# A fused conditioning, two-layer ternary feed-forward and 4-bit rounding kernel: block 1 conditioned inside block 0's first product, and one 8 KB buffer for the small conditioning tiles

## The reference

```
w = weights[conditions];  c = einsum('bct,bcd->bdt', x, w)
ternarize(W): delta = 0.05*max|W|; mask = |W|>delta; alpha = sum(|W| mask)/max(sum(mask),1); alpha*sign(W)*mask
h = gelu(c @ ternarize(W1).T + b1)            # 512 -> 2048
y = h @ ternarize(W2).T + b2                  # 2048 -> 512
scale = max|y|/7 + 1e-8;  q = clip(round(y/scale), -7, 7)*scale
out = x + q
```

## Time and profile before

| | us |
|---|---|
| median of 3 runs | 1014.92 (1014.45 to 1015.22) |
| the profiled execution | 1013.76 |
| its span | 1012.0 |
| block 0's first product begins | 33.08 |
| its second product begins | 66.13 |
| block 1's first product begins | 97.21 |
| the loop's period | 57.12 |
| the maximum of y is known | 954.94 |

### The profile page before, as it was taken

The page is one execution under the profiler, slowest core; times in us unless marked ns, Lnnn a source line. Parts: engine busy times, 40 slices in busy tenths (PEclk is TensorE's granted clock), DMA queues, the critical chain, the costliest instruction groups (busy, mean ns, idle before and its releaser), DMA issues.

```text
span 1012.0 us, 14566 instructions
## 1 busy us (share of the span) xinstructions
PE 928.2 (92%) x5088; PEld 439.1 (43%) x5088; DVE 647.5 (64%) x1025; ACT 546.2 (54%) x688; POOL 145.4 (14%) x187
## 2 busy tenths in 40 slices
PE   2899999999999999999999999999999999999600
PEld 2354444444444444444444444444444444444200
DVE  7999666566667666665667666565666665633492
ACT  5685826455472827446372827446372826535290
POOL 1420030210303030110303030110303030000000
PEclk9999999999999999999999999999999999999855
DMA  9401201111210301121210301121210301105899
GB/s 347 136 9 38 46 11 42 47 47 41 52 41 17 76 10 41 46 47 41 52 41 10 83 10 41 45 48 41 52 41 10 75 18 42 42 0 201 300 394 391
DMA packets 24317, 77.85 MB, mean 77 GB/s; under 512 B 3952, under 2 KB 4080, under 8 KB 23792
## 3 DMA queue, kind: packets, MB, share of 16 engines
q1 hardware_dynamic: 20032, 73.41, 24.1%
q0 software_dynamic: 3840, 3.94, 1.4%
q10 hardware_dynamic: 432, 0.34, 0.1%
HBM read 60.89 MB, written 16.78 MB: 77 GB/s over the span
## 4 chain that ended last, share of the span: by engine, by line
PE 83%; issue 9%; DVE 4%; ACT 1%; DMA 1%; DVEq 0%; POOL 0%; POOLq 0%
PE ps L426 41%; PE ps L436 36%; PE ps L491 3%; PE ps L406 3%; ACT y L680 1%; DVE st L814 1%; DVE wts L1017 1%; DMA condb<-in_itok_B 1%; DVE y L1017 0%; DVE y L833 0%; PE ps L414 0%; PE ps L454 0%; DVE yc L746 0%; DVEq L58 0%; DVE st L697 0%
## 5 line engine op out<-in xcount | busy, mean ns | idle before, releaser
L426 PE MATMUL ps<-yc,wts 128*128 128x512 f16 x2048 | 446.3, 380 | 3.6 <-DVE yc L746 3.6
L436 PE MATMUL ps<-wts 128*128 128x512 f16 x1792 | 391.4, 379 | 0.0
L426 PEld LDWEIGHTS ps<-yc,wts 128*128 128x128 f16 x2048 | 200.7, 98 | 246.8 <-DVE yc L746 4.1
L730 DVE SCALAR_TENSOR_TENSOR wts<-g,st,wts 128x512 f16<-128x512 f32 x256 | 186.3, 749 | 144.0 <-ACT wts L593 142.4
L588 ACT ACTIVATE g<-ps,b1t,st 128x512 f32<-128x512 f32 x256 | 197.9, 773 | 129.0 <-PE ps L426 120.7
L436 PEld LDWEIGHTS ps<-wts 128*128 128x128 f16 x1792 | 173.4, 98 | 204.9
L593 ACT ACTIVATE wts<-g,st 128x512 f16<-128x512 f32 x256 | 180.8, 712 | 0.0
L575 ACT ACTIVATE xs<-yx,st 128x2048 f16<-128x2048 f32 x28 | 56.1, 2002 | 135.5 <-DVE st L764 135.5
L359 POOL PARTITION_ALL_REDUCE st<-st x46 | 22.7, 494 | 672.5 <-DVE st L699 412.7
L343 POOL DMA_INDIRECT wg<-in_L_cond_weights,ids x112 | 110.0, 982 | 41.5 <-issue 29.1
L735 DVE SCALAR_TENSOR_TENSOR y<-ps,st,b2b 128x512 f32 (+1 forms) x56 | 41.6, 747 | 78.9 <-PE ps L436 78.1
(11 more groups left out here) (127 smaller groups left out, 359.3 us busy)
## 6 DMA issues: line engine op xcount, KB each, us to landing
yx<-in_x SPq DMA_DIRECT2D x56, 512.0 KB, 6.2
out<-wts SPq DMA_DIRECT2D x12, 512.0 KB, 14.9
wts<-in_x SPq DMA_DIRECT2D x10, 512.0 KB, 5.6
y<-in_L_ffn_W SPq DMA_DIRECT2D x8, 512.0 KB, 8.6
wts<-in_x SPq DMA_DIRECT2D x4, 1024.0 KB, 5.2
y<-in_L_ffn_W SPq DMA_DIRECT2D x4, 1024.0 KB, 18.5
y<-in_x SPq DMA_DIRECT2D x4, 1024.0 KB, 10.7
out<-y SPq DMA_DIRECT2D x4, 1024.0 KB, 15.3
```

Of the source, the lines that this page charges most:

```text
L426: last = nc.tensor.matmul(psH[:, j % HB, :], T1T[:, j // HC, k, j % HC * P:(j % HC + 1) * P], csp[:, a, k, :], start=(k == 0 and a == 0), ...
L436: last = nc.tensor.matmul(psY[:, r % 2, :], hsp[:, a, j, r * P:(r + 1) * P], T2T[:, j, :], start=(j == 0 and a == 0), stop=(j == HT - 1 an ...
L730: nc.vector.scalar_tensor_tensor(out=hsp[:, 1, j, :], in0=g[:, j % HB, :], scalar=s_h, in1=hsp[:, 0, j, :], op0=ALU.mult, op1=ALU.subtract ...
```

## The change

The diff does this:

- The small buffers (`wg`, `ws`, `condb`, `idx`, `ids`, `idsd`, `twos`) become slices of one buffer `odd` of 8 KB for each partition; in the end it takes block 1 of x, so 13 blocks of x are loaded before the maximum and 3 after. Every later block moves one place.
- Block 1's conditioning on PE stands behind tile 0 of block 0's first product. Its copy goes to a buffer of its own (`cf1`), beside GELU of tiles 3 and 5; ACT's `relu2(0)` stands behind GELU of tile 11. The gathers, `spread_w(1)` and x's load for it come earlier.
- DVE no longer takes the maximum of block 0's x; ACT takes the sum of |x| in each partition in its place (`dump_x`). Two memsets stand ahead of a wait.
- `count2` counts with the masks as the stationary side and one column of `twos` as the moving side: 64 matmuls in place of 16.
- DVE's order beside block 0's two products is new, and `low_x(0, 0)` stands behind the four `max_y` instead of ahead of the four `store_y`.

```diff
-twos = sb("twos", [P, P], FP16)
...
+odd = sb("odd", [P, RT * T], FP32)
+wg = odd[:, 0:BB * C].rearrange("p (b d) -> p b d", b=BB)
+ws = odd[:, BB * C:2 * BB * C].bitcast(FP16).rearrange("p (a b d) -> p a b d", a=2, b=BB)
+odd_i = odd[:, 2 * BB * C:].bitcast(I32)
+condb, idx, ids = odd_i[:, 0:B], odd_i[:, B:2 * B], odd_i[:, 2 * B:2 * B + BB]
+idsd = odd_i[:, 2 * B + BB:2 * B + BB + DIRECT * RT].rearrange("p (b r) -> p b r", b=DIRECT)
+twos = odd[:, 3 * BB * C:3 * BB * C + P // 2].bitcast(FP16)
...
-       10: [(slice(m, m + 1), ALL) for m in (0, 1)],
-       11: [(slice(m, m + 1), ALL) for m in (0, 1)]}
+       11: [(slice(m, m + 1), ALL) for m in (0, 1)],
+       12: [(slice(m, m + 1), ALL) for m in (0, 1)]}
...
-mask1, neg2, dump2 = f16(y[:, 12:14, :, :]), f16(y[:, 4:6, :, :]), f16(y[:, 0:4, :, :])
+mask1, neg2, dump2 = f16(y[:, 12:14, :, :]), f16(y[:, 6:8, :, :]), f16(y[:, 0:4, :, :])
...
+cf1 = y[:, 4, :, :]
+dump_x = hsp[:, 0, 0:RT, :].rearrange("p j r -> p (j r)")
...
-xtail = [place(xs[:, :, :].rearrange("p b t -> p (b t)").bitcast(FP32)),
+xtail = [place(xs[:, :, :].rearrange("p b t -> p (b t)").bitcast(FP32)), place(odd[:, :]),
...
-xhalf = {10: [parts[:, 2, 2:3, :, :], parts[:, 0:2, 3, 0:1, :].rearrange("p w n t -> p n w t")],
-         11: [parts[:, 2, 3:4, :, :], parts[:, 0:2, 3, 1:2, :].rearrange("p w n t -> p n w t")]}
-APART = (6, 8, 9, 10, 11)
+xhalf = {11: [parts[:, 2, 2:3, :, :], parts[:, 0:2, 3, 0:1, :].rearrange("p w n t -> p n w t")],
+         12: [parts[:, 2, 3:4, :, :], parts[:, 0:2, 3, 1:2, :].rearrange("p w n t -> p n w t")]}
+APART = (7, 9, 10, 11, 12)
...
-psC1 = psH[:, 0:2, :].rearrange("p i (k r) -> p (i k) r", k=KT // 2)
-psN1, psN2 = psH[:, HB - 1, :], ps[:, HB, :]
+psN1, psN2 = psH[:, HB - 1, :], ps[:, HB, 0:1]
...
     load_direct(0)
+    load_direct(1)
     load_weight(w2s, W2.rearrange("p j n -> p (j n)"), WCH, w2_loaded)
-    load_direct(1)
...
     sp.wait_ge(c_made, 2 * NB)
-    load_tail(0)
+    for b in range(2):
+        load_tail(b)
     sp.wait_ge(h_summed, NB * HT - HT // 2)
-    load_tail(1)
+    load_tail(2)
     sp.wait_ge(h_summed, NB * HT)
-    for b in range(2, 4):
+    for b in range(3, 5):
         load_tail(b)
...
-    def gather_direct(b):
-        for r in range(RT):
+    def gather_direct(b, tiles):
+        for r in tiles:
...
     pool.wait_ge(idx_made, 1)
-    gather_direct(0)
+    gather_direct(0, range(RT))
+    gather_direct(1, range(0, 2))
...
     all_max(max1_part, 1, m1r, m1, max1_all)
+    gather_direct(1, range(2, RT))
+    pool.wait_ge(x0_summed, 1)
     all_max(xwb_part, 1, xwbr, xwb, xwb_all)
-    gather_direct(1)
     pool.wait_ge(sum1_part, 1)
     nc.gpsimd.partition_all_reduce(rs1r, rs1s, P, RADD).then_inc(sum1_all, 1)
     pool.wait_ge(w_spread, DIRECT)
...
-    all_max(xw_part, 1, xwr, xw, xw_all)
     pool.wait_ge(sum2_part, 1)
     nc.gpsimd.partition_all_reduce(sum2r, sum2, P, RADD).then_inc(sum2_all, 1)
+    all_max(xw_part, 1, xwr, xw, xw_all)
...
     def count2(c):
-        for n in range(WCH):
-            last = nc.tensor.matmul(psN2, twos[:, :], quarter(neg2, c, n), start=(c == 0 and n == 0),
-                                    stop=(c == WCH - 1 and n == WCH - 1))
+        for n in range(QUARTER // P):
+            at = c * QUARTER + n * P
+            last = nc.tensor.matmul(psN2, neg2[:, at:at + P], twos[:, 0:1], start=(c == 0 and n == 0),
+                                    stop=(c == WCH - 1 and n == QUARTER // P - 1))
...
         first(0, j, wait_bank=j >= HB, wait_c=False)
-
-    pe.wait_ge(xdirect_loaded[1], 16)
-    pe.wait_ge(w_spread, 2)
-    condition_direct(1, 0, psC)
-    pe.wait_ge(g_made, HT - 2)
-    condition_direct(1, 1, psC1)
-
+        if j == 0:
+            pe.wait_ge(xdirect_loaded[1], 16)
+            pe.wait_ge(w_spread, 2)
+            condition_direct(1, 0, psC)
+            condition_direct(1, 1, psC0)
+
+    pe.wait_ge(c_copied, 2)
     pe.wait_ge(g_made, HT)
...
         if j == 3 * HC:
-            pe.wait_ge(c_copied, 1)
             for c in range(WCH):
                 count2(c)
...
-    for c in range(6):
+    for c in range(LOADS):
         absolute(c)
+    act.dma_start(b2b[:, :], b2.rearrange("(a n) -> a n", a=1).to_broadcast([P, T])).then_inc(b2_loaded, 16)
     act.wait_ge(diagonal_cleared, 1)
     spread_w(0)
-    for c in range(6, LOADS):
-        absolute(c)
-    act.dma_start(b2b[:, :], b2.rearrange("(a n) -> a n", a=1).to_broadcast([P, T])).then_inc(b2_loaded, 16)
+    act.wait_ge(xdirect_loaded[0], 16)
+    nc.scalar.activation(dump_x, xdirect[0].rearrange("p r t -> p (r t)"), ACT.Abs, accum_out=xwb[:, 0:1])\
+        .then_inc(x0_summed, 1)
     act.wait_ge(delta1_ready, 1)
     act.wait_ge(w1abs_made, LOADS)
-    for c in range(3):
-        relu1(c)
+    relu1(0)
     high_c0(0, psC)
     high_c0(1, psC0)
+    relu1(1)
+    act.wait_ge(c_made, 2)
+    spread_w(1)
+    relu1(2)
     relu1(3)
     act.wait_ge(relu_summed, WCH)
-    hidden(0, lambda j: spread_w(1) if j == 3 else None, wait_c=False)
-
-    act.wait_ge(delta2_ready, 1)
-    act.wait_ge(t1_made, WCH)
-    for side in range(2):
-        relu2(0, side)
-    act.wait_ge(h_split, HT)
-    copy_c_direct(1, 0, psC[:, :, :])
-    copy_c_direct(1, 1, psC1)
-    for side in range(2):
-        relu2(1, side)
-    high_c(1)
-    for c in range(2, WCH):
+
+    def beside_first(j):
+        if j in (3, 5):
+            copy_c_direct(1, (j - 3) // 2, (psC, psC0)[(j - 3) // 2])
+        if j == 11:
+            act.wait_ge(delta2_ready, 1)
+            act.wait_ge(t1_made, WCH)
+            for side in range(2):
+                relu2(0, side)
+
+    hidden(0, beside_first, wait_c=False)
+
+    for c in range(1, WCH):
         for side in range(2):
             relu2(c, side)
+    act.wait_ge(h_summed, HT)
+    high_c(1, cf1)
     high_x(0, 0)
     hidden(1, lambda j: high_x(1, 1) if j == 5 else None)
...
+    nc.vector.memset(wdirect, 0.0).then_inc(diagonal_cleared, 1)
+    nc.vector.memset(twos[:, :], 2.0).then_inc(consts_made, 1)
     dve.wait_ge(cond_loaded, 16)
...
     last.then_inc(idx_made, 1)
-    nc.vector.memset(wdirect, 0.0).then_inc(diagonal_cleared, 1)
-    nc.vector.memset(twos[:, :], 2.0).then_inc(consts_made, 1)
...
     mask_w1(0)
+    dve.wait_ge(wd_gathered[0], 16 * RT)
+    nc.vector.tensor_reduce(xwb[:, 1:2], wg[:, 0:RT, :], AX.XY, ALU.max, apply_absolute_value=True).then_inc(xwb_part, 1)
     mask_w1(1)
-    dve.wait_ge(wd_gathered[0], 16 * RT)
-    nc.vector.tensor_reduce(xwb[:, 1:2], wg[:, 0:RT, :], AX.XY, ALU.max, apply_absolute_value=True)
-    dve.wait_ge(xdirect_loaded[0], 16)
-    nc.vector.tensor_reduce(xwb[:, 0:1], xdirect[0], AX.XY, ALU.max, apply_absolute_value=True).then_inc(xwb_part, 1)
     mask_w1(2)
...
-    nc.vector.tensor_scalar(mr[:, 1:2], pc, float(2 * KT), None, ALU.mult)
+    nc.vector.tensor_scalar(mr[:, 1:2], pc, 2.0 / P, None, ALU.mult)
     mask_w1(3)
     ternary1(0)
     dve.wait_ge(cscale_ready, 1)
     low_c0(0, psC)
     low_c0(1, psC0)
+    dve.wait_ge(n1_counted, 1)
+    nc.vector.tensor_reduce(n1, psN1, AX.X, ALU.add).then_inc(n_read, 1)
+    ternary1(1)
+    ternary1(2)
     dve.wait_ge(relu_summed, WCH)
     nc.vector.tensor_reduce(rs1s, rs1, AX.X, ALU.add).then_inc(sum1_part, 1)
-    dve.wait_ge(n1_counted, 1)
-    nc.vector.tensor_reduce(n1, psN1, AX.X, ALU.add).then_inc(n_read, 1)
     dve.wait_ge(n_read, 1)
...
-    ternary1(1)
+    ternary1(3)
     low_h(0, 0)
-    ternary1(2)
-    low_h(0, 1)
-    low_h(0, 2)
-    max_w2(0)
-    low_h(0, 3)
-    low_h(0, 4)
-    ternary1(3)
-    for c in range(1, WCH):
-        low_h(0, 2 * c + 3)
-        low_h(0, 2 * c + 4)
+    for c in range(WCH):
         last = max_w2(c)
+        low_h(0, 2 * c + 1)
+        if c < WCH - 1:
+            low_h(0, 2 * c + 2)
     link(last)
     nc.vector.tensor_reduce(mx2, wm2, AX.X, ALU.max).then_inc(max2_part, 1)
-    low_h(0, 11)
+    low_h(0, 8)
     dve.wait_ge(max2_all, 1)
     nc.vector.tensor_scalar(dl2, mx2r, THRESHOLD, None, ALU.mult)
     link(nc.vector.tensor_scalar(nd2, mx2r, -THRESHOLD, None, ALU.mult))
     dve.sem_inc(delta2_ready, 1)
+    dve.wait_ge(relu_summed, WCH)
     ternary2(0)
-    for j in range(12, HT):
+    for j in range(9, 12):
         low_h(0, j)
     ternary2(1)
-    max_c(1, link)
+    low_h(0, 12)
     ternary2(2)
+    low_h(0, 13)
+    max_c(1, link, cf1)
+    ternary2(3)
+    for j in range(14, HT):
+        low_h(0, j)
     nc.vector.tensor_scalar(ph0, ph, 1.0 / TOP, None, ALU.mult)
     scale_c(1, link)
     scale_h(1, link)
-    low_c(1)
-    ternary2(3)
-    max_xw(0, 0, DIRECT)
+    low_c(1, cf1)
+    dve.wait_ge(n2_counted, 1)
+    nc.vector.tensor_copy(at2[:, WCH:], psN2).then_inc(n2_read, 1)
     dve.wait_ge(t2_made, WCH)
+    dve.wait_ge(n2_read, 1)
     nc.vector.tensor_reduce(sum2[:, 1:2], at2, AX.X, ALU.add)
     dve.wait_ge(relu2_summed, 2 * WCH)
     nc.vector.tensor_reduce(sum2[:, 0:1], rs2, AX.X, ALU.add).then_inc(sum2_part, 1)
-    scale_xw(0, 0, link)
```

(43 more changed lines are left out.)

## The result

| | before | after |
|---|---|---|
| median, us (12 runs each) | 1013.59 (1013.16 to 1015.22) | 1017.45 (1015.56 to 1019.28) |
| ratio, with its 95% interval | | 1.0033 [1.0024, 1.0042] |
| the profiled execution, its span | 1013.76, 1012.0 | 1016.16, 1014.4 |

The changed kernel is slower by 3.9 us in the medians, and its executions spread over 3.7 us where the old one's spread over 2.1. The profile of one execution shows +2.4 of it.

A forecast was written before the change was run, and what follows sets the result against it. PE's two product lines bound the kernel. Terms -0.1 + 1.86 - 1.59 + 5.3 + 1.86 - 2.5 = +4.8 give 1018.6 us for the profiled execution, 1019.7 as median; likeliest case 1016 to 1022, whole range 1013.5 to 1022.

The forecast's parts named there:

- PE's start: Block 0's first product on PE: starts at 30.2 us, 2.9 us earlier, through DVE's shorter chain to L850.
- the second product's start: Block 0's second product: 66.0 us, only 0.1 earlier, because ACT's two relus stand in front of four GELUs.
- the clock behind that wait: Behind PE's 4.6 us idle ahead of block 0's second product: a fall of the clock, +1.86 us (0 to 1.86).
- the counts: Block 0's counting matmuls: 64 load and one-column pairs at 29 ns take 1.86 us instead of 3.45, -1.59.
- the stop ahead of tile 10: Block 1's first product: late `low_x(0, 0)` delays the load of half 1, so PE stops, +5.3 us (4.3 to 6.3).
- the clock behind the stop: After PE's idle in block 1's first product: another fall of the clock, +1.86 us (0 to 1.86).
- the thirteenth block: At the end: one load of 1.05 MB leaves the stretch of full transfers, -2.5 us (-2.7 to 0).
- rival B: PE stalls as forecast but the clock falls in neither idle: 1016.0 us; chance 0.14.
- rival A: Block 1's first product: the half load is hidden and PE never stops; faster, 1012.5 us; chance 0.17.
- rival C: Weight loads pace the counts at 111 ns a pair: 7.1 us in place of 1.86, 1024.9; chance 0.03.
- rivals D and E: ACT's late x sum holds the all-reduce, 1021.7; or DVE's adds set the end, 1022.2; chance 0.03 each.

The follow-up runs named there:

- the second trace: The changed kernel run again with no edit, on another look at its stop: 1019.34 us, ratio 1.0052 to the kernel before.
- the kernel with the late relus: Changed kernel with x's first-half maximum and scale earlier, `low_x(0, 0)` ahead of the stores, and `relu2(0)` behind the 16 GELUs: 1006.81 us, ratio 0.9926.

## Why the prediction was right

It said slower by 4.8 us; 3.9 were measured. As a time it said 1019.7, and 1017.45 was measured; 1.3 us of this difference is the kernel before, whose median is 1013.59 in 12 runs and was 1014.92 in the three that the forecast was added to. Step by step, in the profiled execution:

| step | predicted | trace | |
|---|---|---|---|
| PE's start | 30.2 | 30.29 | right |
| the second product's start | 66.0 | 64.75 | GELUs 12 to 15 late as said, by less |
| the clock behind that wait | +1.86 | 0 | didn't fall here; did in two experiments |
| the counts | -1.59 | -1.85 | 25 ns a pair, not 29 |
| the stop ahead of tile 10 | +5.3 | +6.59 (5.22 in the second trace) | right, and its place |
| the clock behind the stop | +1.86 | +1.6 (2.2 in the second trace) | right |
| the thirteenth block | -2.5 | -2.8 (2.7 by taking it away) | right |

- That the sizes come this close is in part luck. The profiled execution is 2.4 us slower, half of what was said: the start of the second product was 1.2 us earlier than forecast and the fall of the clock behind it, 1.9, wasn't there, and a late landing gave 1.3 back at the stop. The sign rests on the stop alone, and that is shown.
- The stop was the deciding term, and its derivation held to a tenth of a microsecond where the transfer landed as in the loop: 5.22 against 5.3. The error of the first trace, 1.3 us, is the landing (8.7 us from the split to the maximum, not 7.5), which I had taken as fixed.
- The second product's start was mis-sized by 1.2 us. I took 3.6 us from the sum over W1 to the first GELU from the earlier trace rows, but that stretch holds the 0.68 us of the count's reduction, which I had also charged ahead of it: 2.67 us in the new trace (35.27 to 37.94). The delta of W2 came at 55.4 in place of 56.5 to 57.2, although two low parts stand between the last maximum and it and not one, as I had read. So early, it held ACT no longer: the relus followed GELU 11 and ended at 60.05, not at 61.2. And I named ACT's relus alone as what held the last GELUs; taking them away gave 1.5 us, not the whole wait, because DVE's `ternary2(0)` held them too. That was a second holder close behind the first, which I hadn't looked for.
- The forecast counted on the clock's fall behind an idle of 4.6 us. The idle was 3.09, under the 3.61 of the earlier trace rows, and then the clock fell in two of four traces with this same idle. With a wait of this length the time is no single number, and rival B, in which the clock doesn't fall, was half true in the first trace.
- On rival A: the decision point was put at a split ending 2.1 us behind the product's start. With the split ending 4.5 behind it PE still stopped for 2.29, which puts the end of the stop at 2.2; with the split ahead of it, or 0.5 behind it (the kernel with the late relus), PE didn't stop. A's condition was right, and the changed kernel, at 7.4, doesn't meet it.
- On rival C: a full weight load with one column costs 25 ns, so 64 take 1.60 us and not 7.1. The Trainium skill (TensorE: Matmul & The Clock Gate) gives 107 ns in the section "LDWEIGHTS (loading the stationary operand)" and, in the section "Back-to-back issue gap", a floor of about 25 ns between starts of small matmuls. The pairs here start at that floor, the load included; the 107 ns are near the length of one load's record, 95 to 98 ns, and are no pace.
- On rivals D and E: ACT's sum of x ended at 21.2, and POOL's all-reduce began at 22.96, behind a gather; DVE waited for it for 0.5 us, not 2. Taking the thirteenth block away cost 2.7 us at the end, so DVE's adds don't set it.
- The spread of the changed kernel's runs fits a path that now holds a transfer's landing (7.3 and 8.7 us in two traces) and two waits behind which the clock can fall (1.4 to 2.2 us each time). The kernel with neither stop nor relus spreads over 0.7 us in four runs. The one without the stop but with the relus still spreads over 3.1 in five, so the landing can't be all of it. What makes the spread wasn't shown: 1.3 us of the second trace came in the loop, in five rounds that took 0.1 to 0.4 us longer than 57.12, and PE's stops ahead of tile 10, 0.2 us in two of them, are only a part of that.

## What to carry to other kernels

An operation that frees a buffer for the next load is worth its place in the queue by what the load is for, however idle its own engine looks: here a `low_x` that ended 7.4 us into a product, 3 us of it for maxima that nobody waited for, stopped PE for 5 to 7 us within that product. A cost at one place in the order can be read off the loop, where the same chain runs with known slack (start of the split to wanted tile), and subtracting the two gives the stop before anything is built. When work is taken out from ahead of the bound engine, follow the next wait to all its holders; taking away the first gives only the distance to the second.

## What the runs showed of the hardware that was not expected

- A matmul stream can keep PE busy and still lose the clock: behind 3.2 us of one-column matmuls (128 pairs, PE busy in every window, with records that overlap) the granted clock fell to 0.5 (1.2 GHz) and the next 32 matmuls took 8.75 us instead of 7.07. Behind 1.6 us of them (64 pairs) it stayed at 1.00 in all nine traces that have them.
- One and the same idle of 3.09 us ahead of the second product lowered the clock in two traces (96 matmuls in 22.3 and 22.5 us) and not in two others (20.88). Ahead of the first product an idle of 2.87 us lowered it (x's maximum on DVE: 8 matmuls in 3.24), and idles of 2.39 and 2.16 us (the changed kernel, the doubled counts) didn't (1.90). Around the idle of 2.29 us it fell too, after work had resumed: PE restarted at 115.16, the clock was still 1.00 at 113 to 115, 0.83 at 115 to 116 and 0.50 behind that. With 2.29 us lowering it and 2.39 not, the length of the idle alone doesn't decide.
- A float16 weight load of 128 x 128 with a matmul of one column costs 25 ns when they follow each other: 1.60 us for 64, 3.20 for 128.
